# Flamingo block: keys and queries stored once as three parts, loads that repeat rows, maxima from 64 rows and two heads at a time

## What is computed

```python
q = (query @ Wq + bq).reshape(8, 512, 16, 16)      # query: layernorm of x; k, v from ctx
scores = jnp.einsum('bqhd,bkhd->hbqk', q, k) / np.sqrt(DK)
attn = softmax(scores.reshape(H * Bq, Sq, Sk), axis=0)   # 128 (head, batch) pairs
out = jnp.einsum('hbqk,bkhd->bqhd', attn, v).reshape(Bq, Sq, 256) @ Wo + bo
x = x + tanh(g_xattn[0]) * out
x = x + tanh(g_ffn[0]) * ffn(layernorm(x))          # int8-like fake quantisation, gate/up/down
```

## Time and profile before

| | |
|---|---|
| median of 3 runs | 1045.89 us (1040.85 to 1046.31) |
| the profiled execution | 1039.43 us |
| its span, first to last instruction | 1037.5 us |
| busy PE / VectorE / ScalarE / GpSimd | 797.6 / 903.3 / 644.2 / 518.6 us |
| moved by DMA | 180.98 MB, mean 174 GB/s |
| key loads in `attend` | 256 x 256 KB, 2.8 us from issue to landing (median) |

### The profile page before, as it was taken

How to read it: one execution, slowest core, us unless ns; L and a number is a source line. 1 busy time by engine, 2 the same in 40 slices (tenths; PEclk the granted TensorE clock), 3 DMA queues, 4 the chain that set the end, 5 groups by cost and what they waited for, 6 DMA issues and landing times. The chain is left out here.

```text
span 1037.5 us, 21991 instructions
## 1 busy us (share of the span) xinstructions
PE 797.6 (77%) x8184; PEld 443.3 (43%) x8184; DVE 903.3 (87%) x1428; ACT 644.2 (62%) x981; POOL 518.6 (50%) x330
## 2 busy tenths in 40 slices
PE   2789874777777679998888988988889869167656
PEld 1455541111111245555555555555556548022223
DVE  6679844999999889999989999999999987868968
ACT  3354563999999766555655655655656512467674
POOL 4132330000000019988888998888889877022300
PEclk9898896999999899999999999999999989689979
DMA  9489896564555565585555855577455446000013
GB/s 280 162 280 343 265 346 225 190 213 164 180 217 214 193 178 144 144 269 169 148 163 181 274 139 168 154 215 226 137 171 157 135 164 203 0 1 1 0 41 122
DMA packets 112400, 180.98 MB, mean 174 GB/s; under 512 B 10032, under 2 KB 37296, under 8 KB 112304
## 3 DMA queue, kind: packets, MB, share of 16 engines
q1 hardware_dynamic: 112304, 179.67, 54.5%
HBM read 137.70 MB, written 41.94 MB: 173 GB/s over the span
## 5 line engine op out<-in xcount | busy, mean ns | idle before, releaser
L786 POOL TENSOR_TENSOR e<-e,recip 128x768 f32<-128x768 f32 (+3 forms) x256 | 424.1, 1702 | 72.8 <-DVE recip L830 72.8
L763 ACT ACTIVATE e<-ps_att 128x512 f32<-128x512 f32 x512 | 278.9, 595 | 186.5 <-PE ps_att L698 186.5
L694 PE MATMUL ps_att<-shift,minus 128*128 128x512 bf16 x512 | 200.8, 392 | 21.0 <-DMA arena<-k_stack 8.7
L716 PE MATMUL acc<-e,arena 128*32 128x128 f32 x4096 | 170.1, 284 | 50.5 <-DVE e L798 36.5
L698 PE MATMUL ps_att<-arena 128*128 128x128 bf16 x2048 | 202.3, 222 | 0.0
L812 DVE TENSOR_TENSOR total<-total,e 128x512 f32<-128x512 f32 x240 | 168.0, 700 | 27.7 <-ACT e L763 3.3
L553 ACT ACTIVATE copies<-ps_max 128x1024 bf16<-128x1024 f32 x192 | 178.9, 1037 | 20.2 <-PE ps_max L533 20.2
L698 PEld LDWEIGHTS ps_att<-arena 128*128 128x128 bf16 x2048 | 160.7, 100 | 63.4 <-issue 5.1
L533 PE MATMUL ps_max<-q_head,k_head 128*128 128x512 bf16 x512 | 139.3, 387 | 59.1 <-DVE high L572 20.0
L821 DVE TENSOR_TENSOR total<-total,e 128x512 f32<-128x512 f32 x256 | 177.5, 693 | 2.0 <-ACT e L763 0.2
L716 PEld LDWEIGHTS acc<-e,arena 128*32 128x32 f32 x4096 | 105.0, 111 | 88.4 <-issue 54.0
(11 more groups left out here) (129 smaller groups left out, 858.0 us busy)
## 6 DMA issues: line engine op xcount, KB each, us to landing
arena<-k_stack SPq DMA_DIRECT2D x256, 256.0 KB, 2.8
k_stack<-parts SPq DMA_DIRECT2D x64, 256.0 KB, 3.9
q_stack<-parts SPq DMA_DIRECT2D x64, 256.0 KB, 3.7
k_head<-k_stack SPq DMA_DIRECT2D x16, 1024.0 KB, 5.6
q_head<-q_stack SPq DMA_DIRECT2D x16, 1024.0 KB, 7.8
arena<-q_stack SPq DMA_DIRECT2D x64, 256.0 KB, 4.4
arena<-in_x_dram SPq DMA_DIRECT2D x5, 1024.0 KB, 7.9
arena<-in_ctx_dram SPq DMA_DIRECT2D x4, 1024.0 KB, 6.6
```

The lines of the kernel that those rows point to most:

```text
L694: nc.tensor.matmul(ps[half][:], minus[:], shift_at(qc, kc).to_broadcast([P, HB, P]), start=True, stop=False, skip_group_check=True)
L716: last = nc.tensor.matmul(acc[grp:grp + 32, col:col + P], vpad[:, kc, b, v_col:v_col + 32], e[:, slot(i), b * P:(b + 1) * P], start=False, ...
L763: nc.scalar.activation(e[:, slot(i), half * BANK:(half + 1) * BANK], ps[half][:], ACT.Exp, scale=DK ** -0.5).then_inc(exped, 1)
L786: nc.gpsimd.tensor_tensor(part, part, recip[:, kc % 2, :].rearrange("p (a q) -> p a q", a=1) .to_broadcast([P, share, P]), ALU.mult).then_ ...
```

## The change

- Each of the three parts goes to DRAM once, in `k_parts` and `q_parts` of shape [3, 256, 4, 1024]: three stores a group instead of eight. The weights are no longer permuted; a feature's row is head x 16 + d. The stack's row order is now `TERMS`: key part 0 against query parts 0 to 2, part 1 against 0 to 2, part 2 against 0 and 1, the same eight products.
- A stack is put together by the load. `load_keys` issues three DMAs, on 48, 48 and 32 partitions, whose source repeats each of the head's 16 rows; `load_queries` three with rows of two or three parts interleaved. They stand in `attend` and at the end of `maxima`, where one DMA stood.
- The first part is written straight from PSUM with the bias; the rest is computed from PSUM in one VectorE instruction; the tile `full`, its semaphore and one ScalarE instruction per unit go. PE waits for `rest_ready` before it uses a `psP` buffer again.
- `maxima` uses the products of parts 0 and 1 only, 4 x 16 = 64 rows, and puts one head on rows 0 to 63 and another on rows 64 to 127. One batch and two heads make a unit; the two matmuls of a unit read different halves of the rows. A pair of heads is loaded by eight DMAs of 256 KB on 32 partitions each. The hardware loops are written out.

```diff
+PARTS = 3
+TERMS = ((0, 3), (1, 3), (2, 2))
+ROWS = tuple(sum(n for _, n in TERMS[:t]) * DK for t in range(len(TERMS)))
+def load_keys(queue, dst, k_parts, c, h, done):
+    for (part, n), row in zip(TERMS, ROWS):
+        src = k_parts[part, h * DK:(h + 1) * DK, c, :].rearrange("d (a x) -> d a x", a=1)
+        queue.dma_start(dst[row:row + n * DK, :], src.to_broadcast([DK, n, CT])).then_inc(done, 16)
+def load_queries(queue, dst, q_parts, c, h, done):
+    for (_, n), row in zip(TERMS, ROWS):
+        queue.dma_start(dst[row:row + n * DK, :], q_parts[0:n, h * DK:(h + 1) * DK, c, :].rearrange("r d x -> d r x")
+                        ).then_inc(done, 16)
...
-                        for r, part in enumerate(plan):
-                            sp.dma_start(stack[c, h0:h0 + H // DC, r * DK:(r + 1) * DK, :].rearrange("h d x -> d h x"),
+                        for part in range(PARTS):
+                            sp.dma_start((k_parts, q_parts)[m][part, dc * P:(dc + 1) * P, c, :],
                                          parts[:, u % GB, part, :]).then_inc(stacked[u % GB], 16)
...
                     if u >= 4:
-                        pe.wait_ge(s["full_ready"], u - 3)
+                        pe.wait_ge(s["rest_ready"], u - 3)
...
-                        nc.scalar.activation(full[:, u % UB, :], psP[:, u % 4, :], ACT.Identity,
-                                             bias=bias[:, dc:dc + 1]).then_inc(s["full_ready"], 1)
+                        nc.scalar.activation(parts[:, g % GB, 0, n * BANK:(n + 1) * BANK], psP[:, u % 4, :],
+                                             ACT.Identity, bias=bias[:, dc:dc + 1]).then_inc(s["part1_ready"], 1)
...
-                        nc.vector.tensor_tensor(rest[:, u % UB, :], full[:, u % UB, :],
-                                                parts[:, g % GB, 0, n * BANK:(n + 1) * BANK],
-                                                ALU.subtract).then_inc(s["rest_ready"], 1)
+                        nc.vector.scalar_tensor_tensor(
+                            out=rest[:, u % UB, :], in0=psP[:, u % 4, :], scalar=(bk_s, bq_s)[m][:, dc:dc + 1],
+                            in1=parts[:, g % GB, 0, n * BANK:(n + 1) * BANK], op0=ALU.add, op1=ALU.subtract
+                        ).then_inc(s["rest_ready"], 1)
...
+                def load_pair(hp):
+                    i = hp % 2
+                    for j in range(LANES):
+                        rows = slice((hp * LANES + j) * DK, (hp * LANES + j + 1) * DK)
+                        for part in range(TWO):
+                            at = j * HALF + part * TWO * DK
+                            sp.dma_start(k_head[at:at + TWO * DK, i].rearrange("p c x -> p (c x)"),
+                                         k_parts[part, rows].rearrange("d (a c) x -> d a (c x)", a=1)
+                                         .to_broadcast([DK, TWO, NC * CT])).then_inc(loaded[i], 16)
+                            sp.dma_start(q_head[at:at + TWO * DK, i].rearrange("p c x -> p (c x)"),
+                                         q_parts[0:TWO, rows].rearrange("r d c x -> d r (c x)")).then_inc(loaded[i], 16)
+                load_pair(0)
+                load_pair(1)
+                for hp in range(2, PAIRS):
+                    sp.wait_ge(scored, (hp - 1) * UNITS)
+                    load_pair(hp)
...
                         for j in range(LANES):
-                            b = bp * LANES + j
+                            rows = slice(j * HALF, (j + 1) * HALF)
                             last = nc.tensor.matmul(
-                                ps[:, kc, j * S:(j + 1) * S], k_head[:, i, kc, b * P:(b + 1) * P],
-                                q_head[:, i].rearrange("p c (b q) -> p c b q", q=P)[:, :, b, :], start=True, stop=True)
+                                ps[:, kc, j * S:(j + 1) * S], k_head[rows, i, kc, b * P:(b + 1) * P],
+                                q_head[rows, i].rearrange("p c (b q) -> p c b q", q=P)[:, :, b, :], start=True, stop=True)
...
-                        sp.dma_start(ks[:, nxt % KRING, :], k_stack[nxt // H, nxt % H]
-                                     ).then_inc(k_loaded[nxt % KRING], 16)
+                        load_keys(sp, ks[:, nxt % KRING, :], k_parts, nxt // H, nxt % H, k_loaded[nxt % KRING])
                         if not last and i >= STEPS - H:
                             h = i % H
-                            sp.dma_start(qs[:, h, :], q_stack[bass.ds(qc + 1, 1), h].rearrange("a p x -> (a p) x")
-                                         ).then_inc(q_loaded[h], 16)
+                            load_queries(sp, qs[:, h, :], q_parts, qc + 1, h, q_loaded[h])
```

More of the change, by code:

```diff
@@ L70, with prepare @@
 TB = 4
-def prepare(nc, sem, x, ctx_in, wq, bq, wk, bk, wv, bv, wg, wu, wd, k_stack, q_stack, keep):
+def prepare(nc, sem, x, ctx_in, wq, bq, wk, bk, wv, bv, wg, wu, wd, k_parts, q_parts, keep):
     vpad, wT, wd_T, w_scale, wd_row = keep["vpad"], keep["wT"], keep["wd_T"], keep["w_scale"], keep["wd_row"]
@@ L102, in prepare @@
         tmp = sb("tmp", [P, B])
-        full = sb("full", [P, UB, BANK])
         rest = sb("rest", [P, UB, BANK])
@@ L470, in _, with maxima @@
                     pass
-def maxima(nc, sem, k_stack, q_stack, keep):
+def maxima(nc, sem, k_parts, q_parts, keep):
     shift = keep["shift"]
     LANES = 2
-    GROUPS = B // LANES
+    PAIRS = H // LANES
+    GROUPS = B
     UNITS = GROUPS * NC
@@ L487, in maxima @@
     COPIED = NC - 1
+    HALF = P // LANES
+    TWO = 2
+    HEAD_LOADED = 16 * LANES * TWO * 2
     with ExitStack() as es:
@@ L513, in _ @@
+                load_pair(0)
[3 more added lines that the diff above has]
+                    load_pair(hp)
                 for h in range(H):
                     if h < KRING:
-                        sp.dma_start(keep["ks"][:, h, :], k_stack[0, h]).then_inc(keep["k_loaded"][h], 16)
-                    sp.dma_start(keep["qs"][:, h, :], q_stack[0, h]).then_inc(keep["q_loaded"][h], 16)
+                        load_keys(sp, keep["ks"][:, h, :], k_parts, 0, h, keep["k_loaded"][h])
+                    load_queries(sp, keep["qs"][:, h, :], q_parts, 0, h, keep["q_loaded"][h])
@@ L518, in _ @@
             @block.tensor
             def _(pe):
-                def head(r, i, first):
-                    pe.wait_ge(loaded[i], (r + 1) * 32)
+                for hp in range(PAIRS):
+                    i = hp % 2
+                    pe.wait_ge(loaded[i], (hp // 2 + 1) * HEAD_LOADED)
                     for u in range(UNITS):
-                        bp, kc = u // NC, u % NC
-                        if not (first and bp == 0):
-                            g = (r * 2 + i) * GROUPS + bp
+                        b, kc = u // NC, u % NC
+                        g = hp * GROUPS + b
+                        if g:
@@ L563, in _ @@
                 dve.wait_ge(high_set, 1)
[L565 to L584 removed]
+                for g in range(PAIRS * GROUPS):
+                    if g:
+                        dve.wait_ge(updated, g * 2 - 1)
+                    dve.wait_ge(scored, g * NC + NC)
+                    nc.vector.tensor_tensor(high[:, COPIED, :], ps[:, COPIED, :], high[:, COPIED, :], ALU.max
+                                            ).then_inc(updated, 1)
+                    if g:
+                        dve.wait_ge(updated, g * 2)
+                    dve.wait_ge(copied, g * COPIED + COPIED)
+                    nc.vector.tensor_tensor(high[:, 0:COPIED, :], copies[:, g % RING], high[:, 0:COPIED, :], ALU.max
+                                            ).then_inc(updated, 1)
+                dve.wait_ge(updated, 2 * GROUPS * PAIRS)
                 nc.vector.tensor_tensor(shift[:], high[:, :, 0:S], high[:, :, S:2 * S], ALU.max).then_inc(folded, 1)
@@ L593, in store_sums, with attend @@
                      out_s[rows, :].rearrange("p (r b q) -> p r b q", b=2, q=P)[:, :, b // (B // 2), :]).then_inc(stored, 16)
-def attend(nc, sem, k_stack, q_stack, out_parts, ffn_small, x_first, keep):
+def attend(nc, sem, k_parts, q_parts, out_parts, ffn_small, x_first, keep):
     vpad, shift, ks, qs, out_s = keep["vpad"], keep["shift"], keep["ks"], keep["qs"], keep["out_s"]
@@ L1350, in flamingo_block @@
             keep["shift"] = att.enter_context(nc.sbuf_tensor("shift", [P, NC, S], BF16))
-            prepare(nc, sem, x, ctx_in, wq, bq, wk, bk, wv, bv, wg, wu, wd, k_stack, q_stack, keep)
-            maxima(nc, sem, k_stack, q_stack, keep)
-            attend(nc, sem, k_stack, q_stack, out_parts, (wo, bo, g_x, g_f, clip_x, clip_d),
+            prepare(nc, sem, x, ctx_in, wq, bq, wk, bk, wv, bv, wg, wu, wd, k_parts, q_parts, keep)
+            maxima(nc, sem, k_parts, q_parts, keep)
+            attend(nc, sem, k_parts, q_parts, out_parts, (wo, bo, g_x, g_f, clip_x, clip_d),
                    x[:, 0:P, :].rearrange("b p d -> p b d"), keep)
```

103 lines of the change are left out of this document (22 added, 81 removed).

## The result

The change makes the kernel slower by an eighth: 1177.26 us in the median of 4 runs (1170.99 to 1180.98) against 1043.37 of the kernel before on the same chip, a ratio of 1.1276 with an interval of 1.1242 to 1.1310. The forecast was 1064, the range ended at 1104. The profiled execution took 1170.99 us, its span is 1169.2.

What follows compares the result with a forecast made beforehand. VectorE was taken to set the pace of `attend`, ScalarE and VectorE to fill `maxima`, and stores to end `prepare`. Terms -10 + 2 + 0 + 25 + 3 = +20 on 1039.4 gave 1059.4, put at 1064 us for the runs; range 1034 to 1104.

Steps and rivals of the forecast that it cites:

- Attend, +28: In `attend`, SP's issue of three loads where one stood costs 25 us in query-load steps plus 3 at the sums' stores.
- rival C: In `attend`, issues as dear as the `out_parts` stores' 0.61 us: 65 us in place of 25, kernel 1104; chance 0.15.
- hidden for 208 of the 256 steps: In `attend`, three key-load issues in a row take 1.33 us against 1.8 or more a step, so plain steps lose nothing.
- A: The main forecast: all terms as summed, kernel 1064 us, own range 1048 to 1085; chance 0.52.
- Ring and lead: In `attend`, key buffers absorb 1.6 us and PE's lead over VectorE 2.9 of 12.9 us a chunk, leaving 8.4.
- Prepare, -10: End of `prepare`: fewer stores and a shorter chain bring the first load of `maxima` forward; -10 us (-7 to -14).
- Start of maxima, +2: First pair of heads as eight loads on 32 partitions takes 10.5 us against 8.6: +2 (-1 to +5).
- Maxima, 0: `maxima` itself stays at 181 us, as ScalarE and VectorE stay full and PE's matmuls stay hidden.
- D: `maxima` bound by PE if 64-row matmuls don't run two at a time and clock is 1.2 GHz: +39, 1103; chance 0.08.
- B: In `attend` the issue time stays hidden, the 25 us vanish: -5, about 1038, other ends 1028; chance 0.25.
- Stores of sums, +3: In `attend`, the key load behind the eight stores of sums needs three issues with the lead used up: +3 (0 to 6).

## Why the prediction was wrong

- **What bounded the kernel before.** Right for all three stages: VectorE set the pace of `attend`, and the cover of the loads was what the change spent.
- **Attend, +28: this term failed, at +147.4.** The step is the price of an issue. I took 0.48 "because plain loads of these tensors show it", and kept 0.61 as the bound and rival C; 0.635 is what the rows show, while plain loads of the same sizes take 0.422 (0.465 with the gap). The very reason given for C, a DRAM side of separate rows with repeats, was the right one.
- **"hidden for 208 of the 256 steps": wrong at that price.** 3 x 0.635 = 1.9 us is more than the 1.8 of a step, so no plain step is covered, and the steps without query loads ahead of them gave 46.6 us of the 147.4. C was priced for the 48 steps with queries alone: 65, from 6 x 0.61 = 3.66 us a step less ring and lead, where these steps took up to 4.0 and lost 101. Its sentence that SP "hardly catches up" got no number. Priced over the stage (756 key loads, 144 query loads, 24 stores), 924 issues at 0.61 are 564 us, 89 more than the 475 of `attend`, in place of the 28 of A: C would have stood at 1125, beyond the range. From 0.61 to the mean of 0.668 measured it is another 54. The failure is thus one of size and of scope: issues of SP were the right mechanism, but at their true price they are over the limit everywhere and not in 48 steps.
- **Ring and lead (1.6 and 2.9 us a chunk).** With plain rows at 0.465, `attend` lost 32 us where the working gave 25: for a queue that is over its limit only in places, the working held. The 16 steps that the query loads delay lost 43 us there, and some 11 were won back elsewhere. At 0.635 there is nowhere to win time back.
- **Prepare, -10: -17.7.** The direction and the seam were right. The last third part was to be done at 146.4 and was at 139.3: I credited 3 us of what lay upstream, and it was 10. The shorter chain alone moved the first load by 1.9 of the 17.7 us, as ScalarE then had to wait for buffers that the eight stores still held; with three stores it waited for none, so they are part of the gain within the stage too and not only at its seam. Which of the upstream waits gave the 7 us that I had not credited stays open.
- **Start of maxima, +2: +4.0** (12.7 us against 8.6). The transfer is what lasts: 148 to 156 us shows a DMA share of 1.03 at 210 GB/s, where I had taken 240 from the stores of sums. The stretch, in the columns of the earlier trace rows:

```profile
148.00:156.00 8.00, 0.00 (x0) 0.00 (x0) 0.12 (x1) 0.00 (x0) 0.00 (x0) 0.50 1.03 210
```

The Trainium skill's "SBUF — State Buffer", "Door 1: The DMA port swizzle", has 196 GB/s for partitions 0 to 63 at 1 MiB, which had given +4 for this term. The measured +4.0 and 210 GB/s side with it, though these loads are of 256 KB on 32 partitions each.

- **Maxima, 0: -1.3.** Right, although not at the clock before: the granted clock was 0.51 instead of 0.99, and the overlap of the halves hid it. Of D's two conditions the clock came true and the serial halves did not. B did not occur either; its own sum, 1064 - 25, is 1039 and not 1038.
- **Stores of sums, +3.** This term can't be told apart, since SP is full on both sides of them.

## What to carry to other kernels

When an edit multiplies the DMAs of one queue, add up that queue's issue time over the whole stage, gaps and occasional long issues included, and set it against the stage. A queue over 100% sets the pace everywhere, and rings and leads only bridge short excesses. Take the price of an issue from DMAs of the same form on the DRAM side, not of the same tensor; where none is in the trace, let the dearest form bound the whole stage. Of the ways out, fewer and longer loads with a ring deep enough brought `attend` back to its old pace (472.7 us), and a second queue part of the way (530.1). Only stacks for what is loaded at each step, and parts for what is loaded seldom and spread over the steps, made the kernel faster than before.

## What was not expected of the hardware

- An issue's time went by the form of the source, not by size: in the median 0.592 us for repeated or interleaved rows at 64, 96, 192 and 256 KB alike (0.537 at the least), 0.42 for plain ones directly behind one another, 0.30 to 0.33 for a plain one alone. A plain load directly behind an interleaved one took 0.58:

```profile
575.66 1.82 SPq L47 DMA_DIRECT2D arena<-q_parts  x3
577.53 0.58 SPq L668 DMA_DIRECT2D arena<-k_stack  x1
```

- That price holds while the transfers keep up, as they did in the changed kernel (landings of 2.6 us, DMA share 0.45). In the kernel with one plain load each, eleven issues in a row took 0.82 to 1.65 us from 441 to 456 us, with a DMA share of 0.91 and landings of up to 9.3 us. The issue just ahead of them, and the longest:

```profile
440.72 0.32 SPq L47 DMA_DIRECT2D arena<-k_parts  x1
...
446.54 1.65 SPq L53 DMA_DIRECT2D arena<-q_parts  x1
```

- Some issues of any form last 0.75 to 2 us: in `attend` after the change 37 of 673 loads between 360 and 820 us did, with plain rows 40 of 830. With the second queue 77 of SP's 682 issues in `attend` did. What these single ones wait for stays open.
- The granted clock was 0.50 from 167 us to the end of `maxima` with 64-row matmuls and PE busy for 14.6 of 20 us, where 128-row matmuls with PE busy for 15.4 of 20 had 1.00 in the kernel before. Why it was so, no run shows. The kernel before:

```profile
240.00:260.00 20.00, 15.35 (x59) 3.73 (x57) 20.00 (x15) 20.00 (x23) 0.00 (x0) 1.00 0.54 197
```
